# Choosing each expert's tokens on 128 lanes, and a feed-forward whose token shift is a product

## What is computed

```
h = concat(x[:, :, :128], shift_by_one_token(x[:, :, 128:]))
h = layernorm(h) * lg + lb
a, g = split(h @ w1 + b1)            # 682 each
x = x + (a * gelu(g)) @ w2 + b2
```

```
xn = rmsnorm(x) * norm_weight
logits = xn @ router_weight.T + router_bias        # 2048 x 16
probs = softmax(logits, axis=-1)
_, idx = top_k(logits.T, 128)                      # 128 tokens for each expert
y = gelu(xn[idx] @ fc1.T + b1) @ fc2.T + b2
output[idx] += y * probs[idx], divided by the sum of a token's gates
```

## Time and profile before

| | us |
|---|---|
| median of 3 runs | 2440.4 (2435.73 to 4558.38) |
| the profiled execution, its own time | 2437.84 |
| its span | 2436.0 |
| TensorE busy | 1941.8 (80%) |
| VectorE busy | 1387.2 (57%) |
| ScalarE busy | 1033.5 (42%) |
| GpSimd busy | 521.5 (21%) |

### The profile page before, as it was taken

The page is one execution under the profiler, slowest core; times in us unless marked ns, Lnnn a source line. Parts: engine busy times, 40 slices in busy tenths (PEclk is TensorE's granted clock), DMA queues, the critical chain, the costliest instruction groups (busy, mean ns, idle before and its releaser), DMA issues. The chain is left out here.

```text
span 2436.0 us, 32518 instructions
## 1 busy us (share of the span) xinstructions
PE 1941.8 (80%) x11671; PEld 1219.8 (50%) x11703; DVE 1387.2 (57%) x2241; ACT 1033.5 (42%) x2133; POOL 521.5 (21%) x873
## 2 busy tenths in 40 slices
PE   3778888888799896996999889789996998740495
PEld 1345555555476464763656545356564544420494
DVE  3548888888332794324666523266663328869512
ACT  1238888888411442113665522156563214320131
POOL 2102222222322202222222200122220102120221
PEclk9889999999899898998999989899998999965697
DMA  2143111110000100002000000300000000143295
GB/s 73 61 139 106 36 36 36 36 36 2 1 0 1 53 1 1 1 1 90 1 1 1 8 11 0 102 1 1 1 1 17 0 0 10 36 97 113 86 314 156
DMA packets 103054, 101.37 MB, mean 42 GB/s; under 512 B 33702, under 2 KB 87158, under 8 KB 102774
## 3 DMA queue, kind: packets, MB, share of 16 engines
q1 hardware_dynamic: 99830, 95.05, 12.9%
q0 software_dynamic: 3072, 4.34, 1.0%
HBM read 80.34 MB, written 16.92 MB: 40 GB/s over the span
## 5 line engine op out<-in xcount | busy, mean ns | idle before, releaser
L515 DVE TENSOR_REDUCE negmax<-sps 128x1 f32<-128x1024 f32 x256 | 307.8, 1213 | 21.7 <-PE sps L466 21.0
L559 ACT ACTIVATE prob<-sps,negmax 128x1024 f32<-128x1024 f32 x256 | 286.2, 1118 | 9.0 <-DVE negmax L515 6.4
L475 PE MATMUL sps<-ident,prob 128*128 128x128 f32 x1152 | 180.4, 285 | 56.2 <-ACT prob L559 55.1
L475 PEld LDWEIGHTS sps<-ident,prob 128*128 128x128 f32 x1152 | 133.2, 143 | 144.2 <-ACT prob L559 128.9
L466 PE MATMUL sps<-ks,qs 128*128 128x512 f16 x512 | 162.5, 389 | 21.6 <-DVE ores L535 18.3
L604 POOL TENSOR_TENSOR probT<-probT,after 128x128 f32<-128x128 f32 x256 | 116.5, 455 | 278.8 <-DVE probT L523 191.7
L568 ACT COPY probT<-sps 128x512 f32<-128x512 f32 (+1 forms) x192 | 101.6, 529 | 20.3 <-PE sps L475 20.3
L1296 POOL TENSOR_TENSOR la0qs<-la0qn,la0sin 128x256 f32<-128x256 f32 x64 | 60.3, 973 | 195.9 <-DVE la0qn L1373 195.9
L1296 POOL TENSOR_TENSOR la1qs<-la1qn,la1sin 128x256 f32<-128x256 f32 x64 | 60.3, 973 | 195.2 <-DVE la1qn L1373 195.2
L523 DVE COPY probT<-sps 128x512 f32<-128x512 f32 (+3 forms) x192 | 91.6, 477 | 3.0 <-PE sps L475 3.0
L2055 PE MATMUL r_lgps<-ident,chosen 16*128 16x16 f32 x1 | 0.3, 285 | 112.5 <-DVE chosen L1968 112.5
(11 more groups left out here) (401 smaller groups left out, 4375.6 us busy)
## 6 DMA issues: line engine op xcount, KB each, us to landing
w1e<-in_fc_T SPq DMA_DIRECT2D x16, 1024.0 KB, 6.1
w2e<-in_fc_T SPq DMA_DIRECT2D x16, 1024.0 KB, 9.0
qs<-q_parts SPq DMA_DIRECT2D x128, 64.0 KB, 1.9
ks<-k_parts SPq DMA_DIRECT2D x128, 64.0 KB, 1.9
q_parts<-parts SPq DMA_DIRECT2D x8, 512.0 KB, 3.6
k_parts<-parts SPq DMA_DIRECT2D x8, 512.0 KB, 5.4
token_rows<-r_row SPq DMA_DIRECT2D x4, 544.0 KB, 3.1
mixed<-r_zero SPq DMA_DIRECT2D x1, 2056.0 KB, 9.1
```

Of the source, the lines that this page charges most:

```text
L475: mm = pe.transpose(slots[n % 4][:, at * P:(at + 1) * P], prob[:, n % 3, t * P:(t + 1) * P], ident[:])
L515: dve.tensor_reduce(negmax[:, n % 4:n % 4 + 1], slots[n % 4][:], X, ALU.max, negate=True).then_inc(s.max_done, 1)
L559: act.activation(prob[:, n % 3, :], slots[n % 4][:], ACT.Exp, bias=negmax[:, n % 4:n % 4 + 1], accum_out=rowsum[:, tile % 2, n % QUAD:n % ...
```

## The change

The choice is laid out on all 128 partitions: partition p holds expert p mod 16 and segment p div 16, 256 tokens (`logits`). For that the router's weights are given twice with zeros between (`router_wT`), so that a product fills 32 partitions with two segments, and the bias is repeated. The sixteen rounds run on segments and leave 128 sorted values for each of 128 lanes (`best`) with their places (`where8`). Only the threshold of each expert, its 128th value over all segments, is then looked for: `merge` keeps the greater half of two sorted lists and sorts it again, in two steps from 128 lanes to 32; two 32 x 32 transposes bring the last two lists of an expert together, minima give the threshold `least`. Each lane counts its values over it and not under it; two products with constant matrices (`pick`, from `segment_tables`) add the counts over an expert's lanes and over those ahead of each lane. From them follow how many values a lane gives (`mine`) and at which place of the expert's list they begin (`first`). Seven conditional shifts by 64, 32, ... 1 move each lane's places there, and a product adds the eight lanes of an expert into the list of indices, which is cast into `idxT`.

The weights of the first four experts are issued right behind the zeroing of `mixed`, ahead of the stores of rows. `pick` is loaded with the router's weights in the phase before. The probabilities are written in the changed order of `plg`.

In `gated_ffn` the shift by a token is a product of x0res with `shift`, a matrix of ones beside the diagonal, and with `carry` for the row that comes from the tile before; `late(g)` puts it into the PSUM tile tps[0], from which statistics and scaling read it. The DMAs, `late` in SBUF and the memset go. The root is taken on GpSimd (`pow`) and not on ScalarE. The loop is written out; the next group's statistics follow product 2 and its scaling product 4; the projection of tile 0 waits for each chunk by itself. All signals start from zero. `shift` and `carry` are built on GpSimd in the first local attention.

```diff
+     if l == 0:
+         pool.memset(shift[:], 0.0).then_inc(s.blank, 1)
+         pool.memset(carry[:], 0.0).then_inc(s.blank, 1)
+         pool.wait_ge(s.blank, 2)
+         pool.affine_select(out=shift[:], in_=shift[:], compare_op=ALU.not_equal, fill=1.0,
+                            base=1, pattern=[[-1, P]], channel_multiplier=1).then_inc(s.shift_done, 1)
+         pool.affine_select(out=carry[:, 0:1], in_=carry[:, 0:1], compare_op=ALU.not_equal, fill=1.0,
+                            base=1 - P, pattern=[[-1, 1]], channel_multiplier=1).then_inc(s.shift_done, 1)
...
- late = sb(ph + "late", [P, NT, HALF], F32, c)
  pair = sb(ph + "pair", [P, J, 2, 6], F32, c)
+ mom = sb(ph + "mom", [P, J, 2], F32, c)
+ var = sb(ph + "var", [P, J], F32, c)
+ rs = sb(ph + "rs", [P, J], F32, c)
...
-     for lo, hi in ((0, 112), (112, 127)):
-         sp.dma_start(late[lo + 1:hi + 1, :, :], x0res[lo:hi, :, HALF:D]).then_inc(s.late_in, 16)
-     sp.wait_ge(s.row_zero, 1 + 1)
-     for b in range(B):
-         sp.dma_start(late[0:1, b * TPB + 1:(b + 1) * TPB, :],
-                      x0res[P - 1:P, b * TPB:(b + 1) * TPB - 1, HALF:D]).then_inc(s.late_in, 16)
-
  @block.gpsimd
  def _(pool):
-     pool.memset(late[0:1, :, :], 0.0).then_inc(s.row_zero, 1)
...
+     def inverse_deviation(g):
+         pool.wait_ge(s.moments, g * J + J)
+         pool.tensor_scalar(var[:], mom[:, :, 1], EPS, None, ALU.add).then_inc(s.var_done, 1)
+         pool.wait_ge(s.var_done, g + 1)
+         pool.tensor_tensor(rs[:], var[:], power[:, 0:J], ALU.pow).then_inc(s.rstd_done, 1)
+
+     inverse_deviation(0)
+     for g in range(G):
+         base(g)
+         if g + 1 < G:
+             inverse_deviation(g + 1)
...
+     def statistics(g):
+         if g > 0:
+             dve.wait_ge(s.z_done, g * J)
...
+         dve.wait_ge(s.late_done, g + 1)
+         for j in range(J):
+             dve.bn_stats(pair[:, j, 1, :], tps[0][:, j * P:(j + 1) * P]).then_inc(s.stats, 1)
...
+             dve.tensor_scalar(z[:, j, HALF:D], tps[0][:, j * P:(j + 1) * P], mom[:, j, 0:1], rs[:, j:j + 1],
+                               ALU.subtract, ALU.mult).then_inc(s.z_done, 1)
...
+     statistics(0)
+     normalise(0)
+     for g in range(G):
+         for f in range(NF):
+             gated_product(g, f)
+             if f == 2 and g + 1 < G:
+                 statistics(g + 1)
+             if f == 4 and g + 1 < G:
+                 normalise(g + 1)
+         residual(g)
...
+     def late(g):
+         if g > 0:
+             pe.wait_ge(s.zT_done, g * KD)
+         for j in range(J):
+             t = g * J + j
+             inner = t % TPB > 0
+             mm = pe.matmul(tps[0][:, j * P:(j + 1) * P], shift[:], x0res[:, t, HALF:D], start=True, stop=not inner)
+             if inner:
+                 mm = pe.matmul(tps[0][:, j * P:(j + 1) * P], carry[:], x0res[:, t - 1, HALF:D], start=False, stop=True)
+         mm.then_inc(s.late_done, 1)
...
+     def project(g, j):
+         if g > 0 and j % 2 == 0:
+             pe.wait_ge(s.x_done, g * 2 - 1 + j // 2)
          for f, (f0, n) in enumerate(FCH):
-             pe.wait_ge(s.h_done, 1 + g * NF + max(f - 1, 0))
-             for dst, off in ((pg[f % 2], HID), (pa[f % 2], 0)):
-                 for k in range(KD):
-                     mm = pe.matmul(dst[0:n, :], w1[:, k, off + f0:off + f0 + n], zT[:, k, :],
-                                    start=(k == 0), stop=(k == KD - 1))
-             mm.then_inc(s.ag_done, 1)
-         pe.wait_ge(s.h_done, 1 + g * NF + NF)
-         pe.wait_ge(s.x_done, 1 + g * 2)
+             if j == 0:
+                 pe.wait_ge(s.h_done, g * NF + f + 1)
+             mm = pe.matmul(p3[j // 2][:, j % 2, :], hT[0:n, f, j * P:(j + 1) * P], w2[0:n, f, :],
+                            start=(f == 0), stop=(f == NF - 1))
+         mm.then_inc(s.p3_done, 1)
+
+     late(0)
+     turn(0)
+     for g in range(G):
+         pe.wait_ge(s.zT_done, g * KD + KD)
+         for f in range(NF):
+             hidden(g, f)
+             if f == 1 and g + 1 < G:
+                 late(g + 1)
          for j in range(J):
-             if more and j == J - 1:
+             project(g, j)
+             if j == J - 2 and g + 1 < G:
                  turn(g + 1)
...
+ for r in range(RING):
+     sp.dma_start(w1e[:, r, :, :], io["fc1_T"][r].rearrange("(k p) f -> p k f", p=P)).then_inc(s.next_in, 16)
+     sp.dma_start(w2e[:, r, :, :], io["fc2_T"][r].rearrange("(k p) c -> p k c", p=P)).then_inc(s.next_in, 16)
...
- for r in range(RING):
-     sp.dma_start(w1e[:, r, :, :], io["fc1_T"][r].rearrange("(k p) f -> p k f", p=P)).then_inc(s.next_in, 16)
-     sp.dma_start(w2e[:, r, :, :], io["fc2_T"][r].rearrange("(k p) c -> p k c", p=P)).then_inc(s.next_in, 16)
...
+ for i in range(2):
+     pool.memset(lane[i][:, 0:CAP // 2], 0.0).then_inc(s.zeroed, 1)
...
  dve.wait_ge(s.lgT_out, G)
  for r in range(CAP // 8):
+     e8 = slice(r * 8, r * 8 + 8)
      if r > 0:
          dve.wait_ge(s.removed, r)
-     dve.max(best[:], logitsT[:]).then_inc(s.best_done, 1)
+     dve.max(best[:, e8], logits[:]).then_inc(s.best_done, 1)
      dve.wait_ge(s.best_done, r + 1)
-     if r > 0:
-         dve.wait_ge(s.kept, r)
-     dve.max_index(where8[:], best[:], logitsT[:]).then_inc(s.found, 1)
+     dve.max_index(where8[:, e8], best[:, e8], logits[:]).then_inc(s.found, 1)
      dve.wait_ge(s.found, r + 1)
      if r + 1 < CAP // 8:
-         dve.match_replace(logitsT[:], best[:], logitsT[:], -3.4028235e38).then_inc(s.removed, 1)
-     dve.tensor_copy(chosen[:, r * 8:(r + 1) * 8], where8[:]).then_inc(s.kept, 1)
- dve.wait_ge(s.turned, 1)
- dve.tensor_copy(idxT[:], plg[:, 0, :]).then_inc(s.idx_done, 1)
+         dve.match_replace(logits[:], best[:, e8], logits[:], -3.4028235e38).then_inc(s.removed, 1)
...
+ def merge(level, src, n):
+     dve.tensor_copy(back[0:n, :], src[n:2 * n, ::-1]).then_inc(s.reversed, 1)
+     dve.wait_ge(s.reversed, level + 1)
+     dve.tensor_tensor(mrg[0][0:n, :], src[0:n, :], back[0:n, :], ALU.max).then_inc(s.merged, 1)
+     dve.wait_ge(s.merged, level + 1)
+     for k in range(7):
+         a0, a1 = halves(mrg[k % 2][0:n, :], CAP >> (k + 1))
+         b0, b1 = halves(mrg[1 - k % 2][0:n, :], CAP >> (k + 1))
+         dve.tensor_tensor(b0, a0, a1, ALU.max).then_inc(s.sorted, 1)
+         dve.tensor_tensor(b1, a0, a1, ALU.min).then_inc(s.sorted, 1)
+         dve.wait_ge(s.sorted, level * 14 + 2 * k + 2)
+
+ merge(0, best, 64)
+ merge(1, mrg[1], 32)
+ dve.transpose(blocks[:, 0, :], mrg[1][0:32, :]).then_inc(s.in_blocks, 1)
+ dve.transpose(blocks[:, 1, :], mrg[1][0:32, ::-1]).then_inc(s.in_blocks, 1)
+ dve.wait_ge(s.in_blocks, 2)
+ dve.tensor_tensor(low4[:], blocks[:, 0, :].rearrange("p (b e) -> p b e", e=2 * E)[:, :, 0:E],
+                   blocks[:, 1, :].rearrange("p (b e) -> p b e", e=2 * E)[:, :, E:2 * E], ALU.max).then_inc(s.met, 1)
+ dve.wait_ge(s.met, 1)
+ for i in range(2):
+     dve.tensor_reduce(low[:, i * E:i * E + E], low4[:].rearrange("p b e -> p e b"), X, ALU.min).then_inc(s.low_done, 1)
+ dve.wait_ge(s.low_done, 2)
+ dve.transpose(lowT[:], low[:]).then_inc(s.low_turned, 1)
+ dve.wait_ge(s.low_turned, 1)
+ dve.tensor_reduce(least[0:32, :], lowT[:], X, ALU.min).then_inc(s.least0, 1)
+ dve.wait_ge(s.least0, 1)
+ for q in range(1, 4):
+     dve.tensor_copy(least[32 * q:32 * q + 32, :], least[0:32, :]).then_inc(s.spread, 1)
+ dve.wait_ge(s.spread, 3)
...
+ dve.tensor_scalar(over[:, 0, :], best[:], least[:, 0:1], None, ALU.is_gt).then_inc(s.over_done, 1)
+ dve.tensor_scalar(over[:, 1, :], best[:], least[:, 0:1], None, ALU.is_ge).then_inc(s.over_done, 1)
+ dve.wait_ge(s.over_done, 2)
+ dve.tensor_reduce(cnt[:], over[:], X, ALU.add).then_inc(s.counted, 1)
+ dve.tensor_copy(place[:], where8[:]).then_inc(s.placed, 1)
+ dve.wait_ge(s.counted, 1)
+ dve.tensor_tensor(eq[:], cnt[:, 1:2], cnt[:, 0:1], ALU.subtract).then_inc(s.eq_done, 1)
+ dve.wait_ge(s.summed, 1)
+ dve.tensor_scalar(room[:], sums[:, 2:3], -1.0, float(CAP), ALU.mult, ALU.add).then_inc(s.room_done, 1)
+ dve.tensor_copy(below[:], sums[:, 0:2]).then_inc(s.ahead_done, 1)
+ dve.wait_ge(s.ahead_done, 1)
+ dve.tensor_tensor(ahead[:], below[:, 1:2], below[:, 0:1], ALU.subtract).then_inc(s.ahead_done, 1)
+ dve.wait_ge(s.room_done, 1)
+ dve.wait_ge(s.ahead_done, 2)
+ dve.scalar_tensor_tensor(out=first[:], in0=ahead[:], scalar=room[:, 0:1], in1=below[:, 0:1],
+                          op0=ALU.min, op1=ALU.add).then_inc(s.first_done, 1)
+ dve.scalar_tensor_tensor(out=left[:], in0=ahead[:], scalar=-1.0, in1=room[:], op0=ALU.mult, op1=ALU.add).then_inc(s.left_done, 1)
+ dve.wait_ge(s.first_done, 1)
...
+ def bit(n):
+     k = 6 - n
+     dve.tensor_scalar(bits[:, k:k + 1], first[:], float(1 << k), None, ALU.is_ge).then_inc(s.bits_done, 1)
+
+ def rest(n):
+     k = 6 - n
+     dve.wait_ge(s.bits_done, n + 1)
+     dve.scalar_tensor_tensor(out=first[:], in0=bits[:, k:k + 1], scalar=-float(1 << k), in1=first[:],
```

(39 more changed lines are left out.)

205 lines of the change are left out of this document (124 added, 81 removed).

## The result

The changed kernel takes **2361.0 us** (median of 4 runs, 2358.9 to 2362.5) against 2440.4 us in the runs beside it. The ratio is 0.9684, with a 95% interval of 0.9667 to 0.9701: 3.2% faster, and 2 us from the forecast. One execution of the kernel before took 4558 us and is left out of the ratio as a slow one.

The account below looks back on a forecast made before the run. VectorE choosing tokens alone was taken to bound the kernel for 111.6 us, TensorE pacing the feed-forward; 2437.8 - 70 (choice) + 2 (router) - 12 (feed-forward) = 2357.8, forecast 2359 us as median, range 2345 to 2383 for 8 in 10.

Parts of the forecast that it names:

- The slower rival: In the choice, scans cost by all values of all lanes, a round stays at 7.07 us: 2449 us in all; chance 0.01.
- The chain: Small VectorE operations behind the choice's rounds, from merges to dealing and cast: 18.5 us, low bound 15, high bound 28.
- the shifts: In the choice, seven shifts, each a difference and a multiply-add of 128 values (2 x 0.32 us): 4.5 us.
- The sign of being wrong: One of three named signs, for the choice's small VectorE steps: the forecast is wrong if they lie 0.3 us apart or more.
- The counts by products and back: In the choice, the lanes' counts go through two TensorE products and come back: 1.5 us.
- The store behind the loads: Router phase: first row store, queued behind the weight loads, holds ScalarE's group 2; loses nothing to 7 us, 3 taken.
- smaller logits: Router phase: biased copy of 256 columns instead of 512 and two transposes of four gone, some 0.3 us per group: -1.2.
- The entry: Going into a feed-forward phase: the 16 signals that GpSimd raises by one first go, -1.3 us.
- The start: Feed-forward phase, from entry to first hidden product: 11.6 us instead of 15.4, so -3.8 us a phase.
- the other case: Shift products at the feed-forward's start run at the higher clock level: 1.7 us instead of 3.3, gain 5 instead of 3.8.
- The tails: End of each feed-forward group: five projection chunks cover the 1.62 us wait for the last hT, four times: -6.4 a phase.
- The last gated product: Feed-forward loop: not held by the scalings ahead, margin 0.3 us; the rival that it is held, 2372 us, had chance 0.08.

Follow-up runs that it names:

- after again: The changed kernel, unchanged, measured again beside the follow-up runs: 2370.6 us, ratio 0.9675 to the kernel before.
- Experiment 2: Changed kernel with weight loads behind all row stores, or split between them, or with four row buffers: four buffers worth 3.5 us in the router phase, the others about 2.
- loads_split: Changed kernel with weight loads of experts 0 and 1 ahead of the row stores, 2 and 3 between them: 51.3 us of router phase, median some 7 us below after again.
- experiment 5: GpSimd's sum for group 0 put ahead of the statistics' root, on top of loads_split and of four row buffers: 2364.0 us (0.9658) and 2363.8 us (0.9656).
- experiment 3: Changed kernel with each feed-forward group's second product again waiting for the whole gated product: 2381.3 us, ratio 0.9720 to the kernel before.
- experiment 4: Changed kernel with the shift products of each feed-forward group issued twice: 2380.1 us, ratio 0.9717 to the kernel before.

## Why the prediction was right

2359 was forecast and 2361 came, and the mechanism of each half is the one that was forecast. The last step of the sum holds a slip: 2357.8 for the profiled execution and 2.6 us for the median make 2360.4, and 2359 takes only half of the 2.6. Two smaller ones, 6.7 for twice a merge of 3.3 and 3.3 for fourteen records of 0.25, are worth 0.2 us at most. For the profiled execution 2357.8 stands against 2361.5, so 3.7 us too little. Term by term:

- **The choice, -70 forecast, -68.6 found.** A round was put at 1.47 us and takes 1.51: three scans of 0.41 to 0.43 us at the forecast pace. The slower rival (scans priced by all lanes) is out by the same row. The chain was put at 18.5 and takes 19.3. The term that was mis-sized is the shifts: their steps were put 0.32 us apart and lie 0.39 and 0.40 apart, in the last shift too (2205.26, 2205.65, 2206.05), where neither bit nor rest stands between them; seven shifts cost 5.5 us instead of 4.5. Part of the excess is that the multiply-add itself lasts 0.35 us, where a merge's maximum of as many values lasts 0.28; why the difference, at 0.29, is followed only after 0.40 is open. The sign of being wrong, small steps 0.3 us apart or more, did not come for the smallest: operations of one value lie 0.2 apart, as forecast. The operands with stride 2 cost no more than straight ones: the seven levels of a merge, from halves of 64 values down to every second value, take 0.21 to 0.22 us an operation and 0.385 a level, against the 0.38 forecast. The reversed copy starts 0.26 us ahead of the next operation, under the 0.32 forecast. The counts by products and back were put at 1.5 and take 1.1. By the rule of the Trainium skill, VectorE: DVE Perf Modes, section The TRN2 errata, each small operation pays a fixed latency, estimated from that page at 0.157 us; the operations of one value per lane agree, with 0.15 us each in the timeline of the changed kernel.
- **Router phase, +2 forecast, +2.7 found.** The sum is near by luck, by two errors that cancel. The store behind the loads was forecast to cost 3 us: from ScalarE's rows of group 1 to those of group 2 there are 16.2 us instead of 14.4, so 1.8 (3.0 in after again, with 17.4). The 1.2 us for smaller logits came as 0.2 between groups 0 and 1, and not at all in the last group, where the way from its rows to the first MAX8 grew from 9.3 to 10.2 us (2154.11 to 2164.27), since transposes and router product take 1.97 and 3.44 us there and took 1.30 and 2.95: the clock again, which the sum held constant. Experiment 2 shows that it is the store, and that 2 to 3.5 us of it can be had back. The Trainium skill, DMA: Bandwidth & Descriptors, section Queues, rings and completion order, has descriptors of a ring consumed in ring order; the runs agree in that the store released ScalarE after 5.2 us with all loads ahead of it, and after 3.1 both with half of them, which had run out by then (DMA share 0.00 from 2132 to 2135 in `loads_split`), and with none.
- **Feed-forward, -12 forecast, -14.9 found in its stages, some -15.7 in the phases themselves** (the second, up to the next phase's first record: 1852.80 to 2016.20 before, 1849.66 to 2005.26 after, 7.8 us; the first is taken to gain as much). The entry gained 1.2 (1.3 forecast). The start gained 4.9 where 3.8 was forecast: the step that missed is "TensorE has been idle and is at the lower level". It has just worked for the attention, and the shift products have a granted clock of 1.00, which the forecast had named as the other case: they hold VectorE up for 1.8 us (1850.66 to 1852.50) instead of 3.3. Statistics and root came 0.5 us quicker than forecast, 1.3 and 1.4 us for 1.5 and 1.7, and the eight scalings a full us slower, 3.1 for 2.1 (1855.20 to 1858.32). Two things are in that: GpSimd beside them (experiment 5, 0.7 us), and the shifted half in PSUM, whose reading was put at nothing and which takes 0.40 us for 0.34. The tails gained their 1.6 each (experiment 3), and the shift products cost 1.78, 1.56 and, for the third set with the records of the first, 1.78 again: 5.1 against 5.4 forecast (experiment 4). So -1.2, -4.9, -6.4 and +5.1 make -7.4 of the 7.8 us. The last gated product was not held by the scalings ahead of it: they end at 1885.95, its operand from ScalarE at 1886.42, and it starts at 1886.45; the margin, put at 0.3 us, was 0.5.
- **Not in the sum at all:** +3.1 in the first attention phase, +1.3 in the third, +0.7 in the setup and +0.2 in the tails, 5.3 us in stages whose speed the forecast took as unchanged, and -0.9 in the experts. The feed-forward's extra 2.9 us pay for half of them. That the median then lies 2 us from the forecast, and not 4 or more, is luck.
